# Row statistics of the first stage moved from VectorE to ScalarE, its biases and weights waited for at their use, and a large load held back

## The chip, the cores and the metric

The kernel runs on one core of a Trainium2 chip. The metric is the device time of one execution in microseconds (us). The core has five engines that run their own instruction streams and meet only through semaphores: PE (TensorE, matmul), DVE (VectorE), ACT (ScalarE), POOL (GpSimd) and SP, which here only issues DMA transfers. Each engine executes its stream in order, so an instruction that waits holds up all that stands behind it.

## The reference, cut to what matters

The model has four stages on x of 8 x 512 rows of 256. Only the first two are touched in more than bookkeeping, and the kernel runs both of them as one block, `first_layer`:

```python
x = x + tanh(g_xattn[0]) * L0_xattn(layernorm(x), ctx, ctx)
x = x + tanh(g_ffn[0])   * L0_ffn(layernorm(x))
x = x + tanh(g_xattn[1]) * L1_xattn(ctx, layernorm(x), mask)
x = x + tanh(g_ffn[1])   * L1_ffn(layernorm(x))

def layernorm(x):
    m = mean(x, -1); v = var(x, -1)
    return (x - m) / sqrt(v + 1e-5)

def L0_xattn(q, k, v):            # attention over the 16 heads of one row
    Q = (q @ Wq + bq).reshape(b, s, 16, 16)
    K = (k @ Wk + bk).reshape(b, s, 16, 16)
    V = (v @ Wv + bv).reshape(b, s, 16, 16)
    w = softmax(einsum('bsid,bsjd->bsij', Q, K) / 4)
    return einsum('bsij,bsjd->bsid', w, V).reshape(b, s, 256) @ Wo + bo
```

L0_ffn is a linear layer to 1024 with relu, rounded to 8 bits, and a linear layer back to 256.

## The kernel before, in words

The 4096 rows of x stand in SBUF as the tensor X, 32 tiles (NT) of 128 rows. `first_layer` works in rounds t = -3 to 38, and every engine's program is one loop over the rounds, written out by hand; semaphores count tiles. The order within a round, and how far one engine's round lies ahead of another's, decides who waits. In round t:

- ACT copies the projections of tile t+2 out of PSUM (`xT_copy`, `kv_copy`, `q_copy`, L454 to L468), copies the transposed result of tile t-1 (L472), takes the exponentials of tile t (`exp`, L477 and L478), normalises tile t+3 (L449), does the relu of the feed-forward part (L493), its results (L498 to L504), sums for the next stage (`next_statistics`, L438 to L442), and as the last thing `f_statistics(t - 1)` (L426 to L432): mean and variance of tile t-1 after its first update, by activations with an accumulated sum.
- POOL does `scores(t + 1)`: products of queries and keys in two instructions (L282, L284), in every odd round then `f_deviations` of a pair of tiles (L273, L275: variance to the power -0.5, and the mean times that), and one addition (L291). Then `weighted(t)` (L296), probabilities times values, for which it waits for `exp(t)`.
- DVE sums POOL's products of tile t-1 (L602, `other_values`) and scales them (L606, tensor `a_on`), takes the row maxima of tile t (L584, L586), makes its own share of products (L590, L597, L574, L578) and updates X (L612, L617).
- PE transposes and projects tile t+2 (`qkv`, L315 to L332), transposes `a_on` of tile t-1 (`turn_out`, L315), does the matmuls of the feed-forward part (L366, L377), the output projection (L342, L343), and adds up the scores of tile t+1 (L350 to L355).

POOL runs ahead of ACT: POOL's round t+1 begins as soon as `weighted(t)` is done, while ACT is still in its round t.

The first layernorm needs mean and variance of every tile of the unchanged X. Before, DVE made them in three portions as X landed (`x_stats`, L666 and L555 to L558: tiles 0 to 3, 4 to 15, 16 to 31), and POOL took each portion's power (`x_deviations`, L266, L268). X is loaded in the same three portions by SP (L201). SP issues, in this order: X part 0, four bias rows, context tile 0, the four weights wk, wv, wq, wo, context tile 1, X part 1 (1.5 MB), w1 and w2 (1 MB each), b1, b2, X part 2 (2 MB), and then the context tiles 2, 3 and so on, each held until PE has used the tile two before it (context tile 2: until `qkv(0)` has used tile 0). DVE splits the biases into three bf16 parts (`split_biases`), and ACT issues the transfer that puts the parts on three partitions (tensor bias3, L418). PE began only when all of `w_in` was there, the four weights and bias3.

Of the kernel before, what the change touches and what calls it, by code (L numbers as in the profile page):

```python
# [12 lines left out]
P = 128  # L13
BATCH, SEQ, D = 8, 512, 256
T = BATCH * SEQ
NT = T // P
# [68 lines left out]
def first_layer(nc, x, ctxT, mask, maskT, g_xattn, g_ffn, W, F0, L1, X, tg, ident_f, stats, mu_rs, xs_dram, ahead):  # L85
# [4 lines left out]
    with ExitStack() as ctx:  # L90
# [73 lines left out]
        act_chain, f_means = sem("act_chain"), sem("f_means")  # L164

# [28 lines left out]
        def _(sp):  # L194
# [21 lines left out]
            context(1)  # L216
            x_part(1)
# [32 lines left out]
        def _(pool):  # L250
# [18 lines left out]

            def f_deviations(b):  # L270
                pair = slice(2 * b, 2 * b + 2)
                pool.wait_ge(f_stats, 2 * b + 2)
                pool.tensor_tensor(mu_rs[:, 1, pair], eps_t[:, pair], half[:, pair], ALU.pow).then_inc(f_rstd, 1)  # L273
                pool.wait_ge(f_rstd, b + 1)
                pool.tensor_tensor(shift[:, pair], shift[:, pair], mu_rs[:, 1, pair], ALU.mult).then_inc(f_shift, 1)  # L275
# [24 lines left out]
            x_deviations(1)  # L300
            for t in ROUNDS:
                if t == 0:
                    x_deviations(2)
                if within(t + 1):
                    scores(t + 1, block_of(t, 3))
                elif block_of(t, 3) is not None:
                    f_deviations(block_of(t, 3))
                if within(t):
                    weighted(t)

        @block.tensor
        def _(pe):
# [5 lines left out]
            def qkv(t):  # L318
                pe.wait_ge(xn_done, t + 1)
                turn(xT_ps, ps_T, xn[t % 2], t)  # L320
                pe.wait_ge(c_in[t % 2], 16 * (t // 2 + 1))
                wait(pe, kv_sb, t)
                for c in range(KC):
                    mm = pe.matmul(ps_kv, cT[t % 2][:, c, :], wkv[:, c, :], start=(c == 0), stop=False)
                mm.then_inc(c_used, 1)
                pe.matmul(ps_kv, ones3[:, :], bias3[:, D:3 * D], start=False, stop=True).then_inc(kv_ps, 1)
                pe.wait_ge(xT_sb, t + 1)
                wait(pe, q_copied, t)
                wait(pe, own_made, t)
# [59 lines left out]
            pe.wait_ge(w_in, 5 * 16)  # L389
# [24 lines left out]
        def _(act):  # L414
            act.wait_ge(g_in, 32)
            act.activation(tg[:, :], gl[:, :], ACT.Tanh).then_inc(tanh_done, 1)
            act.wait_ge(bias_split, 1)
            act.dma_start(bias3[:, :], bias_parts[:, :, :]).then_inc(w_in, 16)  # L418
            act.wait_ge(tanh_done, 1)
            steps = Steps(act, act_chain)  # L420

            def f_statistics(t):

                act.wait_ge(y_used, t + 1)
                steps.wait()
                steps.done(act.activation(spare[:, :], X[:, t, :], ACT.Copy, accum_out=sums[:, t:t + 1]))  # L426
                steps.wait()
                steps.done(act.activation(shift[:, t:t + 1], sums[:, t:t + 1], ACT.Copy, scale=-1.0 / D))
                steps.wait()
                steps.done(act.activation(spare[:, :], X[:, t, :], ACT.Square, bias=shift[:, t:t + 1], accum_out=sums[:, t:t + 1]))  # L430
                steps.wait()
                act.activation(eps_t[:, t:t + 1], sums[:, t:t + 1], ACT.Identity, bias=epsilon[:, :], scale=1.0 / D).then_inc(f_stats, 1)  # L432
# [12 lines left out]
            def normalise(t):  # L445

                wait(act, shift_done, 1 + [t in tiles for tiles in PARTS_OF_X].index(True))
                wait(act, xT_ps, t - 1)
                act.activation(xn[t % 2][:, :], X[:, t, :], ACT.Identity, bias=shift[:, t:t + 1],  # L449
                               scale=mu_rs[:, 1, t:t + 1]).then_inc(xn_done, 1)  # L450
# [62 lines left out]
            for t in ROUNDS:  # L513
# [8 lines left out]
                if within(t + 3):  # L522
                    normalise(t + 3)
                if t == -1:
                    f_weights()
# [14 lines left out]
                if within(t - 1):  # L540
                    f_statistics(t - 1)

        @block.vector
        def _(dve):
# [81 lines left out]
            x_stats(1)  # L626
            dve.wait_ge(tanh_done, 1)
            for t in ROUNDS:
# [14 lines left out]
                if t == -2:  # L643
                    x_stats(2)
# [154 lines left out]
def cross_attention(nc, ctxT, mask, maskT, L1, M1, X, tg, ident_f, stats, mu_rs, kept, ahead, routing, xs, out):  # L799
# [3 lines left out]
    with ExitStack() as ctx:  # L803
# [83 lines left out]
        gate_in, x_out, tables = sem("gate_in"), sem("x_out"), sem("tables")  # L887
# [23 lines left out]
        CONSTS = 20  # L911
# [90 lines left out]
        def _(pool):  # L1002
# [5 lines left out]
            def constants():  # L1008
# [9 lines left out]
                pool.iota(iota_i[:, :], pattern=[[1, NE]], base=0, channel_multiplier=0).then_inc(tables, 1)  # L1018
                pool.iota(token[:, :], pattern=[[P, NT]], base=0, channel_multiplier=1).then_inc(tables, 1)
                pool.wait_ge(consts, 16)  # L1020
# [386 lines left out]
        def _(dve):  # L1407
# [118 lines left out]
            def gate_tables():  # L1526
                dve.wait_ge(tables, 2)
# [183 lines left out]
def experts(nc, M1, X, ident_f, routing, xs, out):  # L1711
# [10 lines left out]
    with ExitStack() as ctx:  # L1722
# [50 lines left out]
        with ExitStack() as run:  # L1773
# [49 lines left out]
            labelled, blanks, before_in = sem_("labelled"), sem_("blanks"), sem_("before_in")  # L1823
# [28 lines left out]
            def _(pool):  # L1852
# [34 lines left out]
                for p in range(2):  # L1887
                    pool.memset(yb[p][:, :, :], 0.0).then_inc(blanks, 1)
                pool.wait_ge(blanks, 2)
# [311 lines left out]
```

## Time and profile before

| | us |
|---|---|
| median of 3 runs | 2061.55 |
| lowest and highest | 2059.53, 2062.3 |
| the profiled execution | 2063.94 |
| its span (first to last instruction) | 2062.2 |
| first stage: start to the next stage's first matmuls | 0 to 515 |
| expert stage at the end, bound by PE | 1375 to 2062 |

Over the whole span PE is busy 92%, DVE 75%, ACT 56% and POOL 45%. These are means over stages that are bound by different engines, so they say nothing on the first stage; that is read from stretches of its own. In a row of the timeline the first number is the start from the beginning of the span, the second the length, both in us, and a bracket gives how long the engine was idle before and who released it. "x10" is a number of instructions merged in one row.

### The profile page before, as it was taken

The page shows a single profiled execution, that of the slowest core. Times are in us where ns is not written, and L with a number is a line of the kernel's source. Part 1 is how long each engine was busy: PE and PEld are TensorE (multiplying, and loading weights), DVE is VectorE, ACT ScalarE, POOL GpSimd, SP SyncE. Part 2 cuts the span into 40 slices and gives each one's busy share as a digit, 9 for nine tenths or more (in the row PEclk, how much of TensorE's full clock was granted, in tenths as well). Part 3 has the DMA queues.
Part 4 walks back from the last instruction along what each step waited for, and adds up shares of the span by engine and source line. Part 5 has one row for each costly group of instructions (what it writes and reads, how often), then busy time and mean ns, then how long its engine had stood idle before and what let it go on. Part 6 is the DMA issues. An engine that isn't in the chain of part 4 may idle for free. (4 is left out here: it accounts for less than half of the span.)

```text
span 2062.2 us, 35515 instructions
## 1 busy us (share of the span) xinstructions
PE 1892.7 (92%) x12100; PEld 1339.9 (65%) x12100; DVE 1552.3 (75%) x3251; ACT 1145.8 (56%) x2414; POOL 935.7 (45%) x674
## 2 busy tenths in 40 slices
PE   4899999986889999998999999959999999999998
PEld 2566776664543434443434343449999999999998
DVE  7999999992566677777767678657777777777785
ACT  2356666655336555555555555516665665656563
POOL 6999999981633334343534351023222231222322
PEclk9999999997999999999999999979999999999999
DMA  5222222210425051524242423037666666666662
GB/s 176 114 93 114 91 113 114 108 37 1 116 65 124 27 129 53 123 68 108 68 110 73 104 92 77 19 108 251 238 224 234 229 230 209 226 226 231 231 226 89
DMA packets 138569, 271.45 MB, mean 132 GB/s; under 512 B 13244, under 2 KB 90256, under 8 KB 132499
## 3 DMA queue, kind: packets, MB, share of 16 engines
q1 hardware_dynamic: 127916, 243.63, 37.9%
q0 software_dynamic: 9952, 25.25, 3.3%
q8 instruction: 99, 1.62, 0.3%
q14 instruction: 84, 0.68, 0.1%
q10 hardware_dynamic: 518, 0.27, 0.0%
HBM read 200.12 MB, written 70.47 MB: 131 GB/s over the span
## 5 line engine op out<-in xcount | busy, mean ns | idle before, releaser
L1476 DVE CUSTOM_DVE_ANT_0 x_dump<-x_ps,x_bias_q 128x512 bf16<-128x512 f32 x512 | 353.1, 690 | 103.0 <-PE x_ps L1160 90.1
L1345 ACT ACTIVATE x_PT<-x_ps 128x512 f32<-128x512 f32 x512 | 292.2, 601 | 230.6 <-PE x_ps L1175 227.4
L1989 ACT ACTIVATE X<-m_ps 128x256 f32<-128x256 f32 (+1 forms) x312 | 113.1, 363 | 222.0 <-PE m_ps L1918 219.6
L1160 PE MATMUL x_ps<-x_KS,x_QS 96*128 96x512 bf16 x512 | 198.1, 387 | 23.1 <-DVE x_mx L1476 22.2
L1872 POOL DMA_INDIRECT out_dram<-e_y,e_label x71 | 71.6, 1008 | 321.6 <-DVE e_y L2051 302.2
L1174 PE MATMUL x_ps<-x_bias_k,x_ident_b 128*128 128x512 bf16 x512 | 196.6, 384 | 2.8 <-DMA x_QS<-x_rows 1.7
L1175 PE MATMUL x_ps<-x_QS,x_KS 98*128 98x512 bf16 x512 | 196.5, 384 | 0.0
L1918 PE MATMUL m_ps<-e_x_lo,m_hi 128*128 128x256 f32 (+1 forms) x640 | 180.1, 281 | 4.5 <-issue 4.5
L1918 PE MATMUL m_ps<-e_x_hi,m_hi 128*128 128x256 f32 (+1 forms) x640 | 180.0, 281 | 0.0
L1918 PE MATMUL m_ps<-e_x_hi,m_lo 128*128 128x256 f32 (+1 forms) x640 | 179.9, 281 | 0.0
L2033 DVE TENSOR_TENSOR X<-X,m_ps 128x256 f32<-128x256 f32 (+1 forms) x312 | 114.0, 394 | 83.8 <-ACT X L1989 80.0
L1864 POOL DMA_INDIRECT e_y<-out_dram,e_label x71 | 101.8, 1434 | 164.8 <-DMA out_dram<-e_y,e_label 83.2
L296 POOL TENSOR_TENSOR a_pool_pv<-a_e,a_v 128x2304 f32<-128x2304 f32 x32 | 162.8, 5087 | 16.0 <-ACT a_e L478 16.0
L1918 PE MATMUL m_ps<-e_x_hi,e_hi 128*128 128x256 f32 (+1 forms) x608 | 169.8, 279 | 0.0
L1918 PE MATMUL m_ps<-e_x_hi,e_lo 128*128 128x256 f32 (+1 forms) x608 | 169.5, 279 | 0.0
L1918 PE MATMUL m_ps<-e_x_lo,e_hi 128*128 128x256 f32 (+1 forms) x608 | 169.5, 279 | 0.0
L1768 DVE TENSOR_TENSOR m_lo<-m_raw,m_hi 128x2048 fp32r<-128x2048 f32 x60 | 137.3, 2288 | 28.8 <-ACT m_hi L1764 28.8
L1768 DVE TENSOR_TENSOR e_lo<-m_raw,e_hi 128x2048 fp32r<-128x2048 f32 x57 | 130.4, 2287 | 26.8 <-ACT e_hi L1764 26.8
L1160 PEld LDWEIGHTS x_ps<-x_KS,x_QS 96*128 96x128 bf16 x512 | 50.1, 98 | 135.5 <-DVE x_mx L1476 104.9
L1918 PEld LDWEIGHTS m_ps<-e_x_lo,m_hi 128*128 128x128 f32 x640 | 121.8, 190 | 4.6 <-issue 4.6
L1918 PEld LDWEIGHTS m_ps<-e_x_hi,m_lo 128*128 128x128 f32 x640 | 121.8, 190 | 0.0
L1918 PEld LDWEIGHTS m_ps<-e_x_hi,m_hi 128*128 128x128 f32 x640 | 121.7, 190 | 0.0
(344 smaller groups left out, 5413.5 us busy)
## 6 DMA issues: line engine op xcount, KB each, us to landing
m_raw<-in_L_ffn_w_dram SPq DMA_DIRECT2D x117, 1024.0 KB, 5.1
expert_in<-a_blank SPq DMA_DIRECT2D x34, 1032.0 KB, 4.4
parts<-x_part SPq DMA_DIRECT2D x24, 512.0 KB, 3.8
m_x<-expert_in SPq DMA_DIRECT2D x32, 258.0 KB, 4.9
next_mask_k<-in_maskT_dram SPq DMA_DIRECT2D x32, 256.0 KB, 2.6
next_mask_q<-in_mask_dram SPq DMA_DIRECT2D x29, 256.0 KB, 2.8
x_KS<-parts SPq DMA_DIRECT2D x16, 384.0 KB, 11.3
x_QS<-parts SPq DMA_DIRECT2D x8, 576.0 KB, 6.7
```

The costliest lines, as they stand in the source:

```text
L296: pool.tensor_tensor(heads(pool_pv[:, :], PV_POOL), probabilities(e_[t % 2][:, PV_OWN * H:], PV_POOL), values(v_sb[t % 3][:, :], PV_POOL), ...
L1160: pe.matmul(ps_max[m % 2], QS[b % 2][0:HROWS, h, q * P:(q + 1) * P], KS[b % 2][0:HROWS, h, :], start=True, stop=True).then_inc(s1_ps, 1)
L1174: pe.matmul(ps_st[e % 3], ident_b[:, :], bias_k[b % 2][:, kc, :], start=True, stop=False)
L1175: pe.matmul(ps_st[e % 3], KS[b % 2][:, h, kc * P:(kc + 1) * P], QS[b % 2][0:HROWS + MROWS, h, :], start=False, stop=True).then_inc(st_read ...
L1345: act.activation(PT[unit % 2][:, k, :], ps_st[e % 3], ACT.Exp, scale=DH ** -0.5).then_inc(exp_done, 1)
L1476: dve.tensor_tensor_reduce(out=dump[:, :], in0=ps_max[m % 2], in1=bias_q[b % 2][:, q, :], scale=1.0, scalar=NEG, op0=ALU.add, op1=ALU.max, ...
L1768: eng.tensor_tensor(w_lo[p][n][:, :, :], raw[n][:, :, :], w_hi[p][n][:, :, :].bitcast(F32), ALU.subtract)\
L1864: pool.indirect_dma_start(out=yb[p][:, n, :], out_offset=None, in_=rows, in_offset=tokens(p, n), bounds_check=T - 1, oob_is_err=False).the ...
L1872: pool.indirect_dma_start(out=rows, out_offset=tokens(p, n), in_=yb[p][:, n, :], in_offset=None, bounds_check=T - 1, oob_is_err=False).the ...
L1918: mm = pe.matmul(out, left[a], right[b], start=first and n == 0, stop=last and n == 2)
L1989: act.activation(silu[f % 2][:, 0:wide], ps_h[f % 4][:, 0:wide], ACT.Silu).then_inc(silu_done, 1)
L2033: dve.tensor_tensor(gated[k % 2][:, n, 0:wide], silu[n][:, 0:wide], ps_h[f % 4][:, BLK:BLK + wide], ALU.mult)\
```

## The change

1. PE no longer waits for everything ahead of its loop. It waits for the four weights ahead of the first projection, and for bias3 (its own semaphore now, `bias3_landed`) ahead of the first matmul that uses it.
2. SP holds X part 1, and with it all that stands behind it in its order, until bias3 has landed.
3. DVE makes the statistics of tiles 0 to 3 only. Those of tiles 4 to 31 are made by ACT, tile t+6 as the last thing of round t, for t = -2 to 25 (`row_statistics`: the same four steps as `f_statistics`). POOL takes the power for a pair of tiles, t+4 and t+5, as the first thing of every even round 0 to 26 (`row_deviations`).
4. ACT issues the transfer of bias3 after it has normalised tile 0, where it was before it.
5. In the later stages some semaphores are merged (two iotas count as constants, two memsets count with the iotas).

```diff
@@ SP
             context(1)
+            sp.wait_ge(bias3_landed, 16)
             x_part(1)
@@ POOL
+            def row_deviations(b):
+                pair, n = slice(2 * b, 2 * b + 2), b - TPB // 2
+                pool.wait_ge(row_stats, 2 * n + 2)
+                pool.tensor_tensor(mu_rs[:, 1, pair], eps_t[:, pair], half[:, pair], ALU.pow).then_inc(rstd_done, 1)
+                pool.wait_ge(rstd_done, n + 2)
+                pool.tensor_tensor(shift[:, pair], shift[:, pair], mu_rs[:, 1, pair], ALU.mult).then_inc(shift_done, 1)
...
             x_deviations(0)
-            x_deviations(1)
             for t in ROUNDS:
-                if t == 0:
-                    x_deviations(2)
+                if t % 2 == 0 and TPB <= t + 4 < NT:
+                    row_deviations((t + 4) // 2)
                 if within(t + 1):
                     scores(t + 1, block_of(t, 3))
@@ PE, qkv(t)
+                if t == 0:
+                    pe.wait_ge(w_in, 4 * 16)
...
+                if t == 0:
+                    pe.wait_ge(bias3_landed, 16)
                 pe.matmul(ps_kv, ones3[:, :], bias3[:, D:3 * D], start=False, stop=True).then_inc(kv_ps, 1)
...
             pe.wait_ge(consts, 5)
-            pe.wait_ge(w_in, 5 * 16)
@@ ACT
-            act.wait_ge(bias_split, 1)
-            act.dma_start(bias3[:, :], bias_parts[:, :, :]).then_inc(w_in, 16)
...
+            def row_statistics(t):
+                act.wait_ge(x_in[[t in tiles for tiles in PARTS_OF_X].index(True)], 16)
+                act.wait_ge(f_means, 1)
+                statistics(t, row_stats)
...
             def normalise(t):
-                wait(act, shift_done, 1 + [t in tiles for tiles in PARTS_OF_X].index(True))
+                act.wait_ge(shift_done, 1 if t < TPB else t // 2 - TPB // 2 + 2)
...
+                if t == -3:
+                    act.wait_ge(bias_split, 1)
+                    act.dma_start(bias3[:, :], bias_parts[:, :, :]).then_inc(bias3_landed, 16)
...
                 if within(t - 1):
                     f_statistics(t - 1)
+                if TPB <= t + 6 < NT:
+                    row_statistics(t + 6)
@@ DVE
             x_stats(0)
             split_biases(4, bias_row, bias_rest, bias_parts)
-            x_stats(1)
...
-                if t == -2:
-                    x_stats(2)
```

The order on POOL, from `weighted` of an odd round through the even round behind it to the next odd one. Before:

```order
L296 TENSOR_TENSOR a_pool_pv<-a_e,a_v 128x2304 [waits a_pv_read,a_e_ready]
L282 TENSOR_TENSOR a_pool_qk<-a_q,a_k 128x1536 [waits a_s_ps,a_q_copied]
L284 TENSOR_TENSOR a_pool_qk<-a_q,a_k 128x1280
L291 TENSOR_TENSOR a_pool_qk<-a_pool_qk 128x1024 [waits a_b_made,a_a_made]
L296 TENSOR_TENSOR a_pool_pv<-a_e,a_v 128x2304 [waits a_pv_read,a_e_ready]
```

And in the changed kernel, in which L292, L294, L301 and L306 are these same lines:

```order
L306 TENSOR_TENSOR a_pool_pv<-a_e,a_v 128x2304 [waits a_pv_read,a_e_ready]
L276 TENSOR_TENSOR mu_rs<-a_eps,a_half 128x2 [waits a_row_stats]
L278 TENSOR_TENSOR a_shift<-a_shift,mu_rs 128x2 [waits a_rstd_done]
L292 TENSOR_TENSOR a_pool_qk<-a_q,a_k 128x1536 [waits a_s_ps,a_q_copied]
L294 TENSOR_TENSOR a_pool_qk<-a_q,a_k 128x1280
L301 TENSOR_TENSOR a_pool_qk<-a_pool_qk 128x1024 [waits a_b_made,a_a_made]
L306 TENSOR_TENSOR a_pool_pv<-a_e,a_v 128x2304 [waits a_pv_read,a_e_ready]
```

The pair's power now stands ahead of the scores, behind a wait for `row_stats`, which ACT raises at the end of its previous round.

The order on ACT at the end of an odd round, before:

```order
L438 ACTIVATE a_spare,a_sums<-X 128x256 [waits a_act_chain,a_f_used]
L440 ACTIVATE mu_rs<-a_sums 128x1 [waits a_act_chain]
L442 ACTIVATE a_spare,mu_rs<-X,mu_rs 128x256 [waits a_act_chain]
L426 ACTIVATE a_spare,a_sums<-X 128x256 [waits a_act_chain,a_y_used]
L428 ACTIVATE a_shift<-a_sums 128x1 [waits a_act_chain]
L430 ACTIVATE a_spare,a_sums<-X,a_shift 128x256 [waits a_act_chain]
L432 ACTIVATE a_eps<-a_sums,a_epsilon 128x1 [waits a_act_chain]
L454 ACTIVATE a_xnT<-a_ps 128x256 [waits a_xT_ps]
```

And in the changed kernel:

```order
L446 ACTIVATE a_spare,a_sums<-X 128x256 [waits a_act_chain,a_y_used]
L448 ACTIVATE a_shift<-a_sums 128x1 [waits a_act_chain]
L450 ACTIVATE a_spare,a_sums<-X,a_shift 128x256 [waits a_act_chain]
L452 ACTIVATE a_eps<-a_sums,a_epsilon 128x1 [waits a_act_chain]
L446 ACTIVATE a_spare,a_sums<-X 128x256 [waits a_act_chain,a_f_means,a_x_in1]
L448 ACTIVATE a_shift<-a_sums 128x1 [waits a_act_chain]
L450 ACTIVATE a_spare,a_sums<-X,a_shift 128x256 [waits a_act_chain]
L452 ACTIVATE a_eps<-a_sums,a_epsilon 128x1 [waits a_act_chain]
L474 ACTIVATE a_xnT<-a_ps 128x256 [waits a_xT_ps]
```

A second set of the four steps, on the unchanged tile t+6, stands between `f_statistics` and the next round's first copy.

The order of SP's transfers at the start is the same but for one wait:

```order
L207 DMA a_cT<-in_ctxT_dram 128x2x128
L202 DMA X<-in_x_dram 128x12x256 [waits a_bias3_landed]
L220 DMA a_w<-in_w1T_dram 128x2x1024
L221 DMA a_w<-in_w2T_dram 128x8x256
L222 DMA a_b1c<-in_b_dram 128x8
L223 DMA a_b<-in_b_dram 1x256
L202 DMA X<-in_x_dram 128x16x256
L207 DMA a_cT<-in_ctxT_dram 128x2x128 [waits a_c_used] x3
```

The wait in the second row is the new one; the last row begins with context tile 2.

## Rows read from the trace of the kernel before

**Rows 1.** Windows view, rounds 10 and 11: window, length, busy per engine, granted clock, DMA.

```profile
177.95:205.25 27.30, 26.08 (x142) 19.14 (x141) 26.13 (x25) 17.64 (x55) 25.84 (x10) 1.00 0.22 87
```

**Rows 2.** Timeline of POOL, rounds 9 to 11: start, length, instruction, [idle before <- releaser].

```profile
164.53 5.10 POOL L296 TENSOR_TENSOR a_pool_pv<-a_e,a_v 128x2304 f32<-128x2304 f32 x1
...
169.58 2.81 POOL L282 TENSOR_TENSOR a_pool_qk<-a_q,a_k 128x1536 f32<-128x1536 f32 x1
...
178.43 5.08 POOL L296 TENSOR_TENSOR a_pool_pv<-a_e,a_v 128x2304 f32<-128x2304 f32 x1 [1.22 <-ACT a_e L478]
...
188.55 0.70 POOL L273 TENSOR_TENSOR mu_rs<-a_eps,a_half 128x2 f32<-128x2 f32 x1
...
189.48 2.38 POOL L291 TENSOR_TENSOR a_pool_qk<-a_pool_qk 128x1024 f32<-128x1024 f32 x1
```

**Rows 3.** Timeline of DVE: rounds 10 and 11, the sum of POOL's products.

```profile
173.67 2.55 DVE L602 TENSOR_REDUCE a_ps<-a_pool_pv 128x144 f32<-128x2304 f32 x1
...
187.03 2.55 DVE L602 TENSOR_REDUCE a_ps<-a_pool_pv 128x144 f32<-128x2304 f32 x1
...
189.73 0.42 DVE L606 TENSOR_TENSOR a_on<-a_ps,a_rden 128x256 f32<-128x256 f32 x1
```

**Rows 4.** Timeline of ACT: statistics of round 9, first and last, and round 11's first.

```profile
171.39 0.42 ACT L426 ACTIVATE a_spare<-X 128x256 f32<-128x256 f32 x1
...
172.80 0.29 ACT L432 ACTIVATE a_eps<-a_sums,a_epsilon 128x1 f32<-128x1 f32 x1
...
186.48 0.36 ACT L454 ACTIVATE a_xnT<-a_ps 128x256 f32<-128x256 f32 x1
```

**Rows 5.** Timelines of POOL and ACT, round 25: the same two ends.

```profile
382.96 5.10 POOL L296 TENSOR_TENSOR a_pool_pv<-a_e,a_v 128x2304 f32<-128x2304 f32 x1
...
391.23 0.29 ACT L432 ACTIVATE a_eps<-a_sums,a_epsilon 128x1 f32<-128x1 f32 x1
```

**Rows 6.** Timeline of PE, rounds 10 and 11, around the wait for DVE.

```profile
176.85 0.44 PE L315 MATMUL a_ps<-ident_f,a_on 128*128 128x128 f32 x2 [0.69 <-DVE a_on L606]
...
179.49 0.28 PE L343 MATMUL a_ps<-a_bias,a_ones 3*128 3x256 bf16 x1
...
189.44 0.28 PE L332 MATMUL a_ps<-a_bias,a_ones 3*128 3x256 bf16 x1
...
190.21 0.44 PE L315 MATMUL a_ps<-ident_f,a_on 128*128 128x128 f32 x2 [0.49 <-DVE a_on L606]
```

**Rows 7.** Timeline of PE, rounds 5 and 6, and the granted clock there in the windows view.

```profile
107.53 0.44 PE L315 MATMUL a_ps<-ident_f,a_on 128*128 128x128 f32 x2 [1.46 <-DVE a_on L606]
...
111.76 0.28 PE L343 MATMUL a_ps<-a_bias,a_ones 3*128 3x256 bf16 x1
...
122.24 0.44 PE L315 MATMUL a_ps<-ident_f,a_on 128*128 128x128 f32 x2 [1.17 <-DVE a_on L606]
...
108.00:110.00 2.00, 2.00 (x12) 2.00 (x12) 1.67 (x2) 1.48 (x4) 1.92 (x3) 0.50 0.24 99
...
122.00:124.00 2.00, 1.76 (x15) 1.76 (x16) 1.60 (x4) 1.25 (x4) 1.85 (x2) 1.00 0.76 318
```

**Rows 8.** Timeline of all engines, the start of the kernel.

```profile
10.68 1.30 ACTq L418 DMA_DIRECT2D a_bias<-a_bias_parts  x1
...
16.23 0.66 PE L315 MATMUL a_ps<-ident_f,a_xn 128*128 128x128 f32 x2 [16.23 <-DMA a_bias<-a_bias_parts]
...
26.79 5.32 DVE L666 BATCH_NORM_STATS2 stats<-X 128x6 f32<-128x256 f32 x16 [0.86 <-DMA X<-in_x_dram]
...
33.11 1.88 PE L324 MATMUL a_ps<-a_wkv,a_cT 128*128 128x512 f32 x4
...
42.62 0.27 ACT L477 ACTIVATE a_ps<-a_sm 128x112 f32<-128x112 f32 x1 [3.33 <-DVE a_sm L586]
```

**Rows 9.** DMA view (KB, us from issue to landing), and windows view, last columns DMA share, GB/s.

```profile
next_bias<-a_next_parts SPq DMA_DIRECT2D x3, 1.5 KB, 1.7
...
12.00:22.00 10.00, 5.21 (x12) 2.34 (x12) 5.27 (x27) 2.16 (x6) 1.59 (x1) 1.00 1.08 362
```

More of the change, by code:

```diff
@@ L164, in first_layer @@
         act_chain, f_means = sem("act_chain"), sem("f_means")
+        bias3_landed, row_stats = sem("bias3_landed"), sem("row_stats")
         slices = lambda a, n: a.rearrange("p (d i j) -> p d i j", d=n, i=H)
@@ L416, in _, with statistics @@
             act.activation(tg[:, :], gl[:, :], ACT.Tanh).then_inc(tanh_done, 1)
-            act.wait_ge(bias_split, 1)
-            act.dma_start(bias3[:, :], bias_parts[:, :, :]).then_inc(w_in, 16)
             act.wait_ge(tanh_done, 1)
             steps = Steps(act, act_chain)
+            def row_statistics(t):
+                act.wait_ge(x_in[[t in tiles for tiles in PARTS_OF_X].index(True)], 16)
+                act.wait_ge(f_means, 1)
+                statistics(t, row_stats)
             def f_statistics(t):
                 act.wait_ge(y_used, t + 1)
+                statistics(t, f_stats)
+            def statistics(t, ready):
                 steps.wait()
@@ L431, in f_statistics @@
                 steps.wait()
-                act.activation(eps_t[:, t:t + 1], sums[:, t:t + 1], ACT.Identity, bias=epsilon[:, :], scale=1.0 / D).then_inc(f_stats, 1)
+                act.activation(eps_t[:, t:t + 1], sums[:, t:t + 1], ACT.Identity, bias=epsilon[:, :], scale=1.0 / D).then_inc(ready, 1)
             def next_statistics(t):
@@ L886, in cross_attention @@
         m_ready, m_free, inverted = sem("m_ready"), sem("m_free"), sem("inverted")
-        gate_in, x_out, tables = sem("gate_in"), sem("x_out"), sem("tables")
+        gate_in, x_out = sem("gate_in"), sem("x_out")
         g_stats, g_rstd, g_xn, g_xT, gap, e2_done = (sem(n) for n in ("g_stats", "g_rstd", "g_xn", "g_xT", "gap", "e2_done"))
@@ L909, in wait @@
                 eng.wait_ge(semaphore, count)
-        CONSTS = 20
+        CONSTS = 22
         block = ctx.enter_context(nc.Block())
@@ L1017, in constants @@
                 pool.memset(ones_b[:, :], 1.0).then_inc(consts, 1)
-                pool.iota(iota_i[:, :], pattern=[[1, NE]], base=0, channel_multiplier=0).then_inc(tables, 1)
-                pool.iota(token[:, :], pattern=[[P, NT]], base=0, channel_multiplier=1).then_inc(tables, 1)
-                pool.wait_ge(consts, 16)
+                pool.iota(iota_i[:, :], pattern=[[1, NE]], base=0, channel_multiplier=0).then_inc(consts, 1)
+                pool.iota(token[:, :], pattern=[[P, NT]], base=0, channel_multiplier=1).then_inc(consts, 1)
+                pool.wait_ge(consts, 18)
                 pool.affine_select(out=before_b[:, :], in_=ones_b[:, :], compare_op=ALU.is_gt, fill=0.0,
@@ L1526, in gate_tables @@
             def gate_tables():
-                dve.wait_ge(tables, 2)
+                dve.wait_ge(consts, CONSTS)
                 do(dve.tensor_copy(iota_e[:, :], iota_i[:, :]))
@@ L1822, in experts @@
             g_high, y_left, y_out = sem_("g_high"), sem_("y_left"), sem_("y_out")
-            labelled, blanks, before_in = sem_("labelled"), sem_("blanks"), sem_("before_in")
+            labelled, before_in = sem_("labelled"), sem_("before_in")
             passed = sem_("passed")
@@ L1887, in _ @@
                 for p in range(2):
-                    pool.memset(yb[p][:, :, :], 0.0).then_inc(blanks, 1)
-                pool.wait_ge(blanks, 2)
+                    pool.memset(yb[p][:, :, :], 0.0).then_inc(iotas, 1)
+                pool.wait_ge(iotas, 7)
                 for q in range(ROUND):
```

## The prediction

> **What bounds the kernel now.** The change lives in the first stage, so I read its stretches only. First the windows view over two of its rounds [rows 1]: of 27.30 us PE is busy 26.08, DVE 26.13, POOL 25.84 and ACT 17.64. Three engines are nearly full and ACT has room. Next the timelines of one pair, rounds 10 and 11. POOL sits idle 1.22 us once in the pair, ahead of `weighted(10)` [rows 2]. DVE starts the sum of tile 9 at 173.67 and that of tile 10 at 187.03 [rows 3], though POOL had finished these products at 169.63 and 183.51 [rows 2]: they lie ready for 4.0 and 3.5 us. So DVE sets the pace, and POOL is early by 3.5 us. Last, where ACT stands against POOL: the reader should see that POOL ends round 9 at 169.63, while ACT ends `f_statistics` of its round 9 at 173.09 [rows 2, 4]. In round 25 the same ends are 388.06 and 391.52 [rows 5]. POOL is ahead of ACT by 3.46 us both times, and in the odd rounds between.
>
> At the start the bound is another: PE waits until 16.23 for bias3, and the first exponentials run at 42.62 [rows 8].
>
> **The new wait on POOL (the main term).** In even round E, POOL's first instruction now needs the statistics of tile E+5, and these are the last work of ACT's round E-1. Take E = 10. ACT ends `f_statistics` at 173.09. The four steps took 171.39 to 173.09, 1.70 us [rows 4]; a second set right behind them adds about 1.65, since neighbouring activations overlap a little. It ends at 174.74. POOL has been free since 169.6, so it stands for 5.1 us. It then runs the pair's power, 188.55 to 189.48 or 0.93 us; the three score instructions, 169.58 to 177.21 (178.43 less the idle 1.22) or 7.63 us; and `weighted`, 5.08 us [rows 2]. With 0.06 us for the semaphore, `weighted(10)` ends at 188.44, and DVE starts summing at about 188.47 where it started at 187.03. So of 5.1 us of standing, 1.22 of old idle and the 3.5 of lead absorb most, less the 0.93 of new work, and 1.4 us is left on DVE, which has no slack of its own. ACT's end of the next odd round follows DVE's `a_on` (PE turns it, the output projection, the update, then ACT), so the delay is passed on and each even round adds its own 1.4. From round 8 to round 26 these are 10 rounds: **+14.1 us**. In rounds 0 to 6 the feed-forward part is not complete, ACT ends earlier, and I charge nothing. The bounds of this term: 0 if something lets ACT run ahead, 20 if the early rounds pay too.
>
> **The clock (a second term, from the first).** PE waits for `a_on` 0.69 us in round 10 and 0.49 in round 11 [rows 6]. With the change `a_on(10)` comes 1.4 later while PE's projections before it end at 189.72 [rows 6] plus about 0.15 (ACT's copy at 186.48 starts 1.65 later [rows 4]). The gap becomes 1.75 us. In round 5 a gap of 1.46 us was followed by a granted clock of 0.50, that is 1.2 instead of 2.4 GHz, and in round 6 one of 1.17 was not [rows 7]. With the slow clock, turning `a_on` to the end of the output projection took 107.53 to 112.04, 4.51 us; at the full clock 176.85 to 179.77, 2.92 us [rows 6, 7]. That is 1.6 us on PE ahead of the relu for which ACT waits, hence 1.6 us on ACT's end of the odd round, on which POOL now waits. Once it happens DVE and ACT fall back against POOL's wait and the gap of the next pair is longer. Odd rounds 9 to 25 are 9; I take 7 of them: **+11.2 us**. Bounds: 0 and 9 x 2.0 = 18. The Trainium skill (TensorE: Matmul & The Clock Gate, section "HAM oscillation — how this bites in real kernels") describes a loop whose wait in every tile throws the array back to the slow clock every time; by it all 9 rounds would pay, and the term would be 14.4.
>
> **The start.** ACT issues bias3 at 10.68 for 1.30 us; it landed only when the large loads had gone by, and PE began at 16.23 [rows 8]. Held back, they no longer compete: the smallest transfer of this kind took 1.7 us [rows 9], so it lands between 12.4 and 13.7, and I take 13.0. The Trainium skill (DMA: Bandwidth & Descriptors, "Anatomy of one DMA") gives about 2.0 us of fixed cost; by it the landing would be 12.7 and the sum 0.3 us lower.
> The price stands behind it on SP's queue. X part 1, w1, w2, X part 2 and context tile 2 are 5.9e6 bytes (1.5 + 1 + 1 + 2 + 0.125 times 1024 x 1024), and at the 362 GB/s of the full queues [rows 9] they take 16.3 us. With 13.0 and the 1.7 us that a small transfer takes by itself that is 31.0; for the issue of the first of them and the waits I add 1, and context tile 2 is there at 32. It used to follow X part 2, landed at 26.8 [rows 8]. So the first tiles gain 3 us and more from bias3, and then tile 2 waits for the transfer: PE projects it at 32 instead of 33.11 [rows 8]. But before, DVE's 16-tile statistics (5.32 us, then their aggregation) [rows 8] stood ahead of its scores, and held back PE's query projection of tile 2, the scores and `exp(0)`; that is gone. From this projection, 1.88 us for keys and values [rows 8] and about as much again for biases, queries and ACT's copies make an estimated 4 us at the full clock and 6.5 at the half; PE will have been idle, so I take 5.4. `exp(0)` at 37.5 against 42.62: **-5 us**. Bounds: -2 (slow clock and bias3 at 14) and -7 (full clock, quick landing). The 12-tile statistics also go from DVE, but ran while it waited for the first query projection: nothing. The merged semaphores of the later stages wait for work that was done just ahead anyway: nothing. The start of the next stage follows the end of this one, so the sum goes through in full.
>
> **Sum.** 14.1 + 11.2 - 5 = +20.3 us. Against the profiled execution, 2063.94 us with a span of 2062.2, that is 2084.2; it lay 2.4 over the median of the runs, so the forecast is 2061.55 + 20.3 = 2082.
>
> **Rivals.**
> - *A: POOL's wait without the clock.* The granted clock was 1.00 in rounds 10 and 11 [rows 1] and a gap of 1.17 did no harm; if 1.75 does none either, +14.1 - 5 = +9, 2071 us. Chance 0.27.
> - *B: the clock in all rounds and longer.* Each odd round pays 2.0 and the first pairs stand too: 18 + 18 - 3 = +33, 2094 us. Chance 0.12.
> - *C, the other side: the wait is covered.* If the last statistics come no later than 1.4 us sooner than I have them (POOL's wait below 3.7 us), DVE never waits, and only the start is left: 2061.55 - 5 = 2056.5 us. For it: ACT has 9.7 us of idle in a pair [rows 1]. Against: these idles lie elsewhere in the round, and from the relu to the end ACT runs without a gap. Chance 0.08.
> - *D: the two cancel.* Stall in few rounds, or ACT's idle taking in half of it, and a start of -7: within 0.2%. Chance 0.06.
> - The forecast, 20.3 us within 5 or so: chance 0.47.
>
> **How the numbers follow.** The time is that of the likeliest case. Its own range is 2077 to 2088. The range of 8 in 10 takes in A and stops short of B and of D: 2066 to 2092. A measurement of this kernel tells a change from none at about 0.2%, 4 us. Faster is C with a little of D, 0.09; the same 0.06; slower 0.85.
>
> **What would show it.** In the changed profile: POOL idle 5 us ahead of the power of a pair in every even round from 8 to 26, released by ACT's last statistics step; DVE idle 1.4 us or more ahead of its sum of POOL's products in the round behind; period of a pair 28.7 us or, with slow matmuls in odd rounds, 30.3, and 27.3 again after round 28; PE's gaps ahead of turning `a_on` near 1.75 us and granted clock below 1.00 in that stretch; bias3 landed at 13, context tile 2 at 32, `exp(0)` at 37 to 38. The forecast is wrong if POOL does not stand, if the odd rounds keep the full clock, or if `exp(0)` is not earlier.

## The result, and the profile after

| | before | after |
|---|---|---|
| median, us | 2061.55 (2059.28 to 2063.67, 5 runs) | 2078.60 (2076.12 to 2092.33, 5 runs) |
| ratio after/before | | 1.0096 (95% interval 1.0062 to 1.0129) |
| span of the profiled execution, us | 2062.2 | 2090.4 |
| sum of POOL's products of tile 8 starts | 159.72 | 155.79 |
| of tile 26 | 405.45 | 424.38 |
| of tile 31, the last | 469.14 | 490.54 |
| next stage's first matmul | 515.37 | 537.48 |

The change costs 17.0 us by the medians. (The ratio in the table would be 19.8 us; it takes in the one long execution of 2092.3.) The profiled execution of after is that long one, the slowest of its five (the others lie between 2076.1 and 2079.4), so its own surplus of 28 us isn't what is to be explained; the section on the prediction comes back to that. Inside the first stage the loss is plain: ahead by 3.9 us at tile 8, behind by 18.9 at tile 26 and by 21.4 at tile 31.

First the pair of rounds 10 and 11 after the change, the timeline of all engines. It answers to [rows 2, 3, 4, 6]. Columns: start, length, instruction, [idle before <- what ended it].

```profile
164.06 5.06 POOL L306 TENSOR_TENSOR a_pool_pv<-a_e,a_v 128x2304 f32<-128x2304 f32 x1
...
170.20 0.29 ACT L452 ACTIVATE a_eps<-a_sums,a_epsilon 128x1 f32<-128x1 f32 x1
...
171.79 0.29 ACT L452 ACTIVATE a_eps<-a_sums,a_epsilon 128x1 f32<-128x1 f32 x1
...
172.16 0.71 POOL L276 TENSOR_TENSOR mu_rs<-a_eps,a_half 128x2 f32<-128x2 f32 x1 [3.04 <-ACT a_eps L452]
...
180.71 5.06 POOL L306 TENSOR_TENSOR a_pool_pv<-a_e,a_v 128x2304 f32<-128x2304 f32 x1
...
185.81 2.56 DVE L627 TENSOR_REDUCE a_ps<-a_pool_pv 128x144 f32<-128x2304 f32 x1 [1.80 <-POOL a_pool_pv L306]
...
188.99 0.54 PE L324 MATMUL a_ps<-ident_f,a_on 128*128 128x128 f32 x2 [2.23 <-DVE a_on L631]
...
202.38 0.71 POOL L276 TENSOR_TENSOR mu_rs<-a_eps,a_half 128x2 f32<-128x2 f32 x1 [3.25 <-ACT a_eps L452]
```

Read it from the top. POOL has finished round 9 at 169.12. ACT ends the feed-forward statistics at 170.49 and the added ones at 172.08, and only then does POOL take the pair's power. `weighted(10)` ends at 185.77, and DVE, which before found these products lying ready for 3.5 us [rows 2, 3], waits 1.80 us for them. PE then waits 2.23 us for `a_on(10)`, where it waited 0.49 [rows 6]. From one power to the next it is 30.22 us; the pair took 27.30 [rows 1].

POOL is now held, and its standing adds straight to the pair: 30.22 less 3.25 of standing is 26.97, all of it its own instructions and their small gaps. Before it stood 1.22 us in a pair, for an `a_e`, with 3.5 us of lead. But no single engine sets the new pace. A ring does: POOL works from its power to the end of `weighted(10)` (172.16 to 185.81, 13.65 us, with the short step to DVE), DVE sums and scales (to 188.99, 3.18 us), PE turns `a_on(10)`, and PE and ACT carry it on to ACT's last statistics, for which POOL waits (to 202.38, 13.39 us). The three parts are the 30.22 us of the pair, so what lengthens any of them lengthens every pair.

The windows view of after: the pair, 2 us after PE's gap in round 11, 2 us after its gap in round 17, and round 27. It answers to [rows 1] and [rows 7]. Columns: window, length, busy of PE, PEld, DVE, ACT, POOL, granted clock, DMA share, GB/s.

```profile
172.16:202.38 30.22, 27.82 (x141) 20.52 (x140) 26.27 (x26) 20.57 (x66) 26.67 (x13) 0.94 0.20 80
...
189.00:191.00 2.00, 2.00 (x10) 2.00 (x11) 1.63 (x3) 1.42 (x4) 2.00 (x2) 0.55 0.15 58
...
279.70:281.70 2.00, 2.00 (x16) 1.96 (x17) 1.63 (x3) 1.58 (x5) 2.00 (x2) 1.00 0.02 8
...
427.00:429.00 2.00, 1.44 (x9) 1.44 (x10) 1.51 (x4) 0.93 (x4) 2.00 (x2) 0.78 1.01 421
```

The full clock of the pair [rows 1] has become 0.94: after the gap of 2.23 us the granted clock was 0.55, close to the lower level of 1.2 GHz. After the gap in round 17, which was 2.24 us long (row below), it stayed at 1.00. From sum to sum of the even tiles 8 to 26 the pairs last 30.02, 30.20, 30.24, 30.17, 28.68, 30.21, 30.19, 30.17 and 28.71 us: seven with the slow clock (0.94 over the whole pair) and two without.

The timeline of after once more, round 17 and, ahead of it, the start, which answers to [rows 8].

```profile
9.71 0.66 PE L324 MATMUL a_ps<-ident_f,a_xn 128*128 128x128 f32 x2 [9.71 <-ACT a_xn L469]
...
10.79 1.30 ACTq L546 DMA_DIRECT2D a_bias<-a_bias_parts  x1
...
12.79 0.37 SPq L202 DMA_DIRECT2D X<-in_x_dram  x1
...
13.94 0.60 PE L339 MATMUL a_ps<-a_bias,a_ones 3*128 3x512 bf16 x1
...
32.01 3.64 PE L335 MATMUL a_ps<-a_wkv,a_cT 128*128 128x512 f32 x4 [3.34 <-DMA a_cT<-in_ctxT_dram]
...
37.49 0.26 ACT L497 ACTIVATE a_ps<-a_sm 128x112 f32<-128x112 f32 x1
...
46.14 2.55 DVE L627 TENSOR_REDUCE a_ps<-a_pool_pv 128x144 f32<-128x2304 f32 x1
...
279.61 0.44 PE L324 MATMUL a_ps<-ident_f,a_on 128*128 128x128 f32 x2 [2.24 <-DVE a_on L631]
```

SP, which waits for bias3, issues X part 1 at 12.79. PE starts at 9.71 instead of 16.23, then has to wait for context tile 2 until 32.01, and projects it at the slow clock (3.64 us for what took 1.88 [rows 8]). The first exponentials run at 37.49, and the first sum of POOL's products at 46.14 instead of 51.55.

### The profile page after: what moved, and what is told of

Same layout as the page of the kernel before. It is cut to its first block and busy times, and to the rows that moved or that the text cites. A ratio compares the mean times of both kernels' runs of the same rounds, so it can differ in the third digit from the quotient of the medians.

```text
span 2090.4 us, 35676 instructions
## 1 busy us (share of the span) xinstructions
PE 1916.0 (92%) x12100; PEld 1353.0 (65%) x12100; DVE 1539.2 (74%) x3191; ACT 1188.2 (57%) x2582; POOL 939.2 (45%) x698
## 5 line engine op out<-in xcount | busy, mean ns | idle before, releaser
L306 POOL TENSOR_TENSOR a_pool_pv<-a_e,a_v 128x2304 f32<-128x2304 f32 x32 | 162.3, 5071 | 1.2 <-ACT a_e L498 1.2
L1078 POOL TENSOR_TENSOR x_rest<-x_full,x_part 128x512 f32<-128x512 f32 x28 | 32.4, 1159 | 201.9 <-ACT x_part L1355 201.9
## 6 DMA issues: line engine op xcount, KB each, us to landing
x_KS<-parts SPq DMA_DIRECT2D x16, 384.0 KB, 11.2
```

The source lines that it names most:

```text
L306: pool.tensor_tensor(heads(pool_pv[:, :], PV_POOL), probabilities(e_[t % 2][:, PV_OWN * H:], PV_POOL), values(v_sb[t % 3][:, :], PV_POOL), ...
```

## The experiments

All times are medians; a ratio is to the kernel before, measured beside it on the same chip. The first four experiments ran on one chip, where the kernel before took 2060.91 us, and the last four on another, where it took 2062.63. A difference to the changed kernel compares runs made at different times, so a few us of it mean little. Rounds, tiles and `sum(t)` (DVE's start on POOL's products of tile t) are as above.

**1. The power taken later (e1_power_later).** The changed kernel, but POOL takes the pair's power behind the two score products of the round.

```diff
-            def scores(t, block):
+            def scores(t, block, rows=None):
...
                 if block is not None:
                     f_deviations(block)
+                if rows is not None:
+                    row_deviations(rows)
                 pool.wait_ge(a_made, t + 1)
...
-                if t % 2 == 0 and TPB <= t + 4 < NT:
-                    row_deviations((t + 4) // 2)
+                rows = (t + 4) // 2 if t % 2 == 0 and TPB <= t + 4 < NT else None
                 if within(t + 1):
-                    scores(t + 1, block_of(t, 3))
+                    scores(t + 1, block_of(t, 3), rows)
```

> The changed kernel with one edit: in even rounds POOL takes the pair's power after its two score products instead of ahead of them. Theory (POOL's wait for ACT's last work of the round before is what costs): the products take 5.1 us, as long as POOL stood, so the wait is gone, DVE sets the pace again at 27.3 us a pair, PE's gap ahead of turning a_on is 0.5 to 0.7 us again and its clock stays up; only the start's gain is left, 2061.5 - 5 = 2056.5 us. Rival 1 (the added work costs: 1.65 us on ACT a round and 0.93 on POOL a pair): the pair stays at 28.7 or more, about 2075. Rival 2 (part of the loss is the later stages, not the first): 2063 or more although the pair is 27.3.

It took 2052.41 us, ratio 0.9958 (0.9944 to 0.9972): 26 us under the changed kernel, and under the kernel before. The timeline of POOL and ACT, round 10:

```profile
165.05 2.40 POOL L294 TENSOR_TENSOR a_pool_qk<-a_q,a_k 128x1280 f32<-128x1280 f32 x1
...
167.10 0.29 ACT L453 ACTIVATE a_eps<-a_sums,a_epsilon 128x1 f32<-128x1 f32 x1
...
167.47 0.71 POOL L276 TENSOR_TENSOR mu_rs<-a_eps,a_half 128x2 f32<-128x2 f32 x1
...
171.14 5.08 POOL L308 TENSOR_TENSOR a_pool_pv<-a_e,a_v 128x2304 f32<-128x2304 f32 x1 [0.36 <-ACT a_e L499]
```

The same instruction, 5.2 us later in POOL's program, waits for nothing: ACT ends at 167.39, POOL is there at 167.47. Only 0.08 us lie between, but 0.36 of old idle stands behind. The windows view of two of its rounds shows the old pair and the full clock, with all the added work in it:

```profile
165.78:193.10 27.32, 26.21 (x141) 19.11 (x140) 26.16 (x27) 20.61 (x67) 26.77 (x13) 1.00 0.22 88
```

So the loss is the place of the wait and not ACT's 3 us or POOL's 0.93 us of work in a pair. I had expected 2056.5, and it was better by 4. Of these the start gives 2.3 (`sum(8)` at 152.43, 7.3 us ahead of before, not 5), and most of that is the clock and not the edit: context tile 2 came as late as in the changed kernel (31.93), but PE projected it in 1.98 us instead of 3.64. The rest I can't place.

**2. The statistics one round earlier (e2_round_earlier).** The power stays in front; ACT takes the row statistics one tile further ahead.

```diff
-                if TPB <= t + 6 < NT:
+                if t <= 0 and TPB <= t + 6:
                     row_statistics(t + 6)
+                if t >= 0 and t + 7 < NT:
+                    row_statistics(t + 7)
```

> The changed kernel with ACT's row statistics one tile further ahead (tiles 6 and 7 both in round 0, from then on tile t+7 in round t); POOL's power stays the first instruction of the even round, and ACT and POOL do just the same work. Theory (the lead, not the work): the statistics are there a round before they are asked for, POOL does not stand, pair 27.3 us, 2056 to 2058 us. Rival (work): no better than the changed kernel, 2078. If it lies between, ACT's extra set in round 0 costs at the start.

2054.17 us, ratio 0.9965 (0.9950 to 0.9979). The timeline of ACT and POOL, rounds 8 to 10:

```profile
155.38 0.29 ACT L452 ACTIVATE a_eps<-a_sums,a_epsilon 128x1 f32<-128x1 f32 x1
...
165.57 0.71 POOL L276 TENSOR_TENSOR mu_rs<-a_eps,a_half 128x2 f32<-128x2 f32 x1
```

The last value that this power needs was made 9.9 us before, at the end of round 8. POOL takes the power at once, and from `sum(6)` on the pairs last 27.3. Two edits that share nothing but the lead of ACT over POOL remove the same loss.

**3. The clock kept (e3_clock_kept).** In odd rounds PE runs three matmuls more ahead of turning `a_on`, on a buffer that is overwritten afterwards; POOL's wait stays.

```diff
+                if t % 2 == 1 and 9 <= t <= 27:
+                    pe.wait_ge(h_act, FC * block_of(t, 5) + 4)
+                    for _ in range(3):
+                        pe.matmul(ps_h[:, 0:PAIR], ident_f[:, :], wkv[:, 0, 0:PAIR], start=True, stop=True)
```

> The changed kernel with three matmuls of the identity added on PE ahead of turning a_on, in the odd rounds 9 to 27, into a PSUM bank that is free there; their result is overwritten. They fill most of the gap in which PE waits. Theory (two terms, wait and clock): POOL still stands, all pairs take 28.7 us instead of 28.7 in two and 30.2 in seven, first stage ends about 11 us sooner than in the changed kernel, about 2067 us. Rival (the long pairs are not the clock's): pairs stay at 30.2 and the time at 2078, or longer by the matmuls.

2067.32 us, ratio 1.0036 (1.0022 to 1.0051), 11.3 us under the changed kernel. The timeline of POOL, DVE and PE, then the windows view of one pair:

```profile
169.68 0.71 POOL L276 TENSOR_TENSOR mu_rs<-a_eps,a_half 128x2 f32<-128x2 f32 x1 [1.69 <-ACT a_eps L456]
...
183.31 2.56 DVE L631 TENSOR_REDUCE a_ps<-a_pool_pv 128x144 f32<-128x2304 f32 x1 [1.28 <-POOL a_pool_pv L306]
184.69 1.56 PE L408 MATMUL a_ps<-a_wkv,ident_f 128*128 128x256 f32 x6
...
186.50 0.44 PE L324 MATMUL a_ps<-ident_f,a_on 128*128 128x128 f32 x2 [0.25 <-DVE a_on L635]
...
198.38 0.71 POOL L276 TENSOR_TENSOR mu_rs<-a_eps,a_half 128x2 f32<-128x2 f32 x1 [1.69 <-ACT a_eps L456]
```

```profile
183.31:212.00 28.69, 27.71 (x147) 20.14 (x146) 26.23 (x26) 20.74 (x66) 26.70 (x13) 1.00 0.21 84
```

The filler (the row of 1.56 us; the profile counts the three matmuls as six) stands where PE was idle, the clock is 1.00, and every pair from `sum(6)` to `sum(26)` lasts 28.7 us. POOL stands 1.69 us, and 28.69 less 1.69 is again 27.0. This divides the loss: POOL's wait makes 27.3 into 28.7, and the clock makes 28.7 into 30.2, through 1.55 us more of standing on POOL. In the ring only one part has changed. POOL's takes 13.63 us (169.68 to 183.31) and DVE's 3.19, as in the changed kernel, but from turning `a_on(10)` to the next power it is 11.88 (186.50 to 198.38) instead of 13.39: the slow clock costs 1.51 us on the way through PE and ACT.

**4. The wait alone (e4_wait_only).** The kernel before, and nothing added but a wait of POOL for ACT's feed-forward statistics of the round before.

```diff
+                if t % 2 == 0 and 2 <= t <= 26:
+                    pool.wait_ge(f_stats, t - 1)
                 if within(t + 1):
                     scores(t + 1, block_of(t, 3))
```

> The kernel before with one wait more and no work: in even rounds 2 to 26 POOL first waits until ACT has ended f_statistics of the round before. Theory: POOL stands 3.5 us in each from round 8 on, less than its 1.2 us of idle and the 3.5 us its products lie ready, so DVE never waits: 2061.5, same within 0.2%. The wait costs only from 4.7 us of standing on. Rival (every wait on POOL is passed on): 10 times 2 us or more, 2080.

2061.92 us, ratio 1.0008 (0.9994 to 1.0023): no change. The timeline of POOL and DVE, round 10:

```profile
173.63 2.80 POOL L282 TENSOR_TENSOR a_pool_qk<-a_q,a_k 128x1536 f32<-128x1536 f32 x1 [1.22 <-ACT a_eps L434]
...
181.23 5.07 POOL L296 TENSOR_TENSOR a_pool_pv<-a_e,a_v 128x2304 f32<-128x2304 f32 x1
...
187.49 2.55 DVE L604 TENSOR_REDUCE a_ps<-a_pool_pv 128x144 f32<-128x2304 f32 x1
```

POOL waits for ACT in each pair, yet DVE doesn't: the products end at 186.30, 1.2 us ahead of the sum, where they were 3.5 ahead [rows 2, 3]. The 3.5 us of standing that I expected didn't come: POOL stands 1.22 us in a pair, as before, only ahead of another instruction. Once it is held in each pair it isn't 3.5 us early at the next one. A wait that ends 1.65 us sooner (my estimate of ACT's second set) and carries no 0.93 of work behind it costs nothing. The threshold of rival C exists, and the change lies beyond it.

**5. The statistics alone (e5_statistics_only).** Only the move of the row statistics; bias3, PE's waits and SP's queue as before.

```diff
             context(1)
-            sp.wait_ge(bias3_landed, 16)
             x_part(1)
...
             act.activation(tg[:, :], gl[:, :], ACT.Tanh).then_inc(tanh_done, 1)
+            act.wait_ge(bias_split, 1)
+            act.dma_start(bias3[:, :], bias_parts[:, :, :]).then_inc(bias3_landed, 16)
...
             pe.wait_ge(consts, 5)
+            pe.wait_ge(w_in, 4 * 16)
+            pe.wait_ge(bias3_landed, 16)
```

> Part 3 of the change alone: the statistics on ACT and POOL as in the changed kernel, but the start as before (X part 1 not held, PE waits for weights and bias3 ahead of its loop, ACT issues bias3 first). Theory (pairs cost what the changed kernel's cost, and nearly all of the start's gain is DVE's freed statistics, not the bias): exp(0) between 31 and 38 us where the changed kernel has 37.5, pairs 28.7 to 30.2, total 2074 to 2079. Rival (the hold and the early bias make the gain): exp(0) near 42, total 2083.

2085.51 us, ratio 1.0107 (1.0087 to 1.0126), 7 us over the changed kernel. My expectation missed. The timeline of POOL, ACT and DVE at its start:

```profile
34.54 0.81 POOL L275 TENSOR_TENSOR mu_rs<-a_eps,a_half 128x2 f32<-128x2 f32 x1 [4.31 <-ACT a_eps L451]
...
36.67 0.41 ACT L497 ACTIVATE a_e<-a_sm 128x256 f32<-128x256 f32 x1
...
43.15 5.02 POOL L305 TENSOR_TENSOR a_pool_pv<-a_e,a_v 128x2304 f32<-128x2304 f32 x1
...
48.20 2.56 DVE L623 TENSOR_REDUCE a_ps<-a_pool_pv 128x144 f32<-128x2304 f32 x1 [3.01 <-POOL a_pool_pv L305]
```

The first exponentials are even a little earlier than in the changed kernel (36.67 against 37.67). But POOL gets its first power at 34.54 instead of 31.34, with `scores(1)` behind it, and `sum(0)` starts at 48.20 instead of 46.14. The new wait bites at the start too, and the first exponentials are not the measure of it. That gives 2.1 us; the first stage ends 2.0 us later than in the changed kernel, and its pairs are the same (30.11 to 30.24, and two of 28.70). The other 5 us of the 7 between the medians I can't place, and they may be none: the two were measured at different times, each beside its own runs of the kernel before, and the intervals of their ratios overlap (1.0087 to 1.0126 and 1.0062 to 1.0129). The profiled executions of the two stand the other way round (spans of 2085.7 and 2090.4).

**6. Experiment 1 without SP's wait for bias3 (e6_later_no_hold).**

```diff
-            sp.wait_ge(bias3_landed, 16)
```

> The kernel with the power taken behind the products (the first experiment, 2052.4 us), with SP's wait for bias3 ahead of X part 1 taken out. Theory (the hold costs, since context tile 2 queues behind all the held loads and exp(0) follows it): context tile 2 lands at 27 instead of 32, exp(0) runs at 31 to 33 instead of 35.8, total 2048. Rival (the hold helps, since bias3 lands at 16 without it and the first projections are 3 us later): exp(0) at 36 or later, total 2052 or more.

2053.57 us, ratio 0.9957 (0.9944 to 0.9970), the same as with the wait (0.9958). In the first stage it is ahead of experiment 1: `sum(0)` at 42.59 against 44.37, and the next stage's first matmul at 506.69 against 508.48. Here bias3 loses less by the large loads than they lose by being held. In the total the 1.8 us don't show.

**7. Experiment 1 with context tiles 2 and 3 ahead of X part 2 (e7_later_contexts_first).**

```diff
+            context(2)
+            context(3)
             x_part(2)
             for t in range(2, NT):
-                context(t)
+                if t > 3:
+                    context(t)
```

> The same kernel as in the first experiment, with context tiles 2 and 3 issued ahead of X part 2 (2 MB) instead of behind it. Theory (context tile 2 is what exp(0) waits for): it lands by 27, PE projects tile 2 as soon as it has added up the scores of tile 0, at 28.3, and ACT, busy with the weights' casts to 31.3, is the next to hold exp(0): at 33 to 34 instead of 35.8; total 2050. Rival (something else holds it): exp(0) stays at 35.8.

2051.03 us, ratio 0.9938 (0.9921 to 0.9956), the lowest median of all: 27.6 us under the changed kernel. From experiment 1, whose interval overlaps, it isn't told apart with certainty. Its timeline, PE and ACT at the start:

```profile
26.79 1.88 PE L339 MATMUL a_ps<-a_wkv,a_cT 128*128 128x512 f32 x4
...
33.13 0.26 ACT L501 ACTIVATE a_ps<-a_sm 128x112 f32<-128x112 f32 x1
```

Tile 2 is projected 5.2 us sooner than in the changed kernel, without a wait and at the full clock, and `exp(0)` comes 4.4 us sooner than there and 2.6 sooner than in experiment 1 (35.75).

**8. The start alone (e8_start_only).** Parts 1, 2 and 4 of the change: bias3 and the weights waited for at their use, SP held, bias3 issued after tile 0 is normalised. The row statistics stay on DVE and POOL, and the later stages are as before.

```diff
             context(1)
+            sp.wait_ge(bias3_landed, 16)
             x_part(1)
...
+                if t == 0:
+                    pe.wait_ge(w_in, 4 * 16)
...
+                if t == 0:
+                    pe.wait_ge(bias3_landed, 16)
...
+                if t == -3:
+                    act.wait_ge(bias_split, 1)
+                    act.dma_start(bias3[:, :], bias_parts[:, :, :]).then_inc(bias3_landed, 16)
                 if t == -1:
                     f_weights()
```

> Parts 1, 2 and 4 of the change alone: the statistics stay on DVE and POOL as in the kernel before. Theory (the held X parts now stand ahead of DVE's statistics, and those ahead of its scores): DVE's 12 tiles run at 19.8 to 25, its scores of tile 0 behind them, the 16 tiles at 31.5 to 38, exp(0) at 45 to 48 instead of 42.6, pairs 27.3, total 2064 to 2067. Rival (the early bias gains by itself): exp(0) near 39, total 2058.

2065.73 us, ratio 1.0018 (1.0004 to 1.0032). The timeline of DVE and ACT at the start:

```profile
19.63 4.02 DVE L672 BATCH_NORM_STATS2 stats<-X 128x6 f32<-128x256 f32 x12 [8.93 <-DMA X<-in_x_dram]
...
31.34 5.33 DVE L672 BATCH_NORM_STATS2 stats<-X 128x6 f32<-128x256 f32 x16 [2.61 <-DMA X<-in_x_dram]
...
47.17 0.27 ACT L480 ACTIVATE a_ps<-a_sm 128x112 f32<-128x112 f32 x1 [3.31 <-DVE a_sm L592]
```

With the loads held, DVE waits for X, and its 16-tile statistics start at 31.34 instead of 26.79 [rows 8]: `exp(0)` is 4.6 us later than before. Of that 3.4 us are left at `sum(8)`. By themselves these three parts of the change lose; they gain only together with the statistics taken off DVE. At `sum(0)` the statistics alone are 3.35 us ahead of before (experiment 5), and all parts together 5.41. Part 5, the merged semaphores, was not run alone.

## Why the prediction was right, and where it wasn't

- **The new wait on POOL, +14.1.** Right in place, cause and size: from `sum(7)` to `sum(26)` experiment 3, which keeps the clock up, takes 14.0 us more than before (273.03 against 259.07). A pair without the clock's part lasts 28.7 us in experiment 3 and twice in the changed kernel, 1.4 over the 27.3 before, in the ten even rounds 8 to 26; from experiment 1 to experiment 3, which differ in the place of the wait and the filler, it is 14.9 us. Experiments 1, 2 and 4 show that it is the lead that counts. One reading of it was wrong: I said that POOL would stand 5.1 us in every pair. It stands 1.7 us, or about 3.2 where the clock falls (2.56 and 3.04 in the first two of these pairs). I had reckoned 5.1 against a POOL that is 3.46 us ahead of ACT. Once it is held it no longer gets that far ahead, and 5.1 less 3.46 is the 1.7 that is seen. The delay handed on was right all the same, since lead and old idle were taken off.
- **The clock, +11.2.** Right in mechanism and near in size: seven of nine pairs paid 1.5 us, and from `sum(7)` to `sum(26)` the changed kernel takes 10.3 us more than experiment 3. (The 11.3 us between the two medians hold the start and the tail as well.) That it would be seven of nine I had from no row: the count was luck. I forecast gaps of 1.75 us, growing once the clock has fallen, and so they did. The first (for tile 8) was 1.75 and the one behind each pair at full clock 1.73 and 1.88 (tiles 18 and 26), the others 2.2. The loop of the Trainium skill (TensorE: Matmul & The Clock Gate, section "HAM oscillation — how this bites in real kernels"), in which each round pays, would have given 14.4; two rounds of this trace didn't pay, at gaps as long as the others (last section).
- **The tail, 0.** Too low. The gap for tile 26 (1.88 us) brought the clock down in round 27 too (0.78 in the windows above). From `sum(26)` to `sum(28)` it took 28.42 us and not 27.3, and 1.4 us more came by the last tile: +2.5. These 1.4 us can't be charged to POOL's wait. From `sum(29)` to `sum(30)` the granted clock was 0.73 where it was 0.85 before, and it was 0.73 too, with the same 1.2 us or more, in experiments 4 and 8, in which DVE doesn't wait for POOL once behind tile 0.
- **The start, -5.** Right in size and in its steps: context tile 2 at 32.01 (forecast 32), `exp(0)` at 37.49 (37.5), and 5.4 us ahead at `sum(0)`. bias3 landed by 12.79, 2.0 us after its issue at 10.79, where I had taken 2.3. The 2.0 us that the prediction quotes from the Trainium skill (DMA: Bandwidth & Descriptors, section "Anatomy of one DMA") agree with that, though the section is on transfers issued by GpSimd and ACT issues this one. The 5.4 us from context tile 2 to `exp(0)` were a choice between 4 at the full and 6.5 at the slow clock, and that they came out is in part luck. In experiments 1 and 3, whose edits don't touch these rounds' PE work, the same wait of 3.3 us was followed by a projection of 1.98 us instead of 3.64, and `exp(0)` was there 3.8 us after the tile, at 35.7. The reason I gave for bias3's part doesn't hold either, since experiments 6 and 8 show that the hold by itself costs. And I hadn't seen why `exp(0)` was quite so late before: DVE's low half of the first feed-forward weights, right ahead of the first softmax, took 4.39 us instead of the 2.28 it takes now (last section). The sum isn't touched by that, because it starts from the measured 42.62; after the change DVE is done with it at 30.83, ahead of context tile 2.
- **The sum, +20.3.** The first stage of the profiled execution ends 21.4 us later: -5.3 up to tile 7, +24.2 from there to tile 26 (forecast 25.3) and +2.5 in the tail. By the medians it is +17.0. The sentence that the sum goes through in full is true of the start of the next stage (+22.1), but the second stage doesn't last equally long each time. From its first matmul to the expert stage's first cast the profiled executions took 871.3 us before, 877.2 after, and between 866.1 and 873.6 in the experiments, none of which changes its work. Before's 871.3 lies 3 to 5 us over the five shortest (866.1 to 868.4). A forecast from one profiled execution is uncertain by these 3 to 5 us at least.
- **From one execution to another.** The granted clock goes with the difference between executions. Added up over windows of 5 us, the second stage ran about 37 to 42 us at the lower level in the five shortest executions and 45 to 58 us in the five others, after's 58 being the most. Take off half of that time as an estimate of what it cost, and all ten last 846 to 849 us. The long profiled execution of after fits this: its mean granted clock is 0.963, that of the other four 0.968 to 0.970, and span times clock, an estimate of the length at full clock, is 2010 to 2014 us in all five. Why the clock falls more often in one execution than in another stays open, and so does how the 17 us of the medians divide over the stages, since only the profiled execution has a trace.
- **The rivals.** A (no clock, 2071) falls by the granted clock of 0.55 and by experiment 3, B by the two pairs at the full clock and by rounds 2 to 6, where POOL stood 1.28 us at most and DVE didn't wait for it; C by DVE's 1.80 us of idle.

## What to carry to other kernels

When work is moved to an engine with room, the room is not the question: look at when its result is ready against when the reader's in-order queue comes to it. Here the same work, read 5 us later in that queue or made a round earlier, turned a loss of 17 us into a gain of 7 to 8.5. If the wait closes a ring of engines, the pair lasts as long as the ring, and every delay in it counts in full. Where the delay opens a gap on PE, look at the granted clock after it: it took the price of a pair from 1.4 us to 2.9.

## What the runs showed of the hardware

**DVE and POOL side by side.** The timeline of the kernel before, then of the changed kernel, at the instructions of DVE and POOL that met at the start:

```profile
36.85 2.79 POOL L282 TENSOR_TENSOR a_pool_qk<-a_q,a_k 128x1536 f32<-128x1536 f32 x1
...
37.40 4.39 DVE L647 TENSOR_TENSOR a_w_lo<-a_w,a_w_hi 128x2048 fp32r<-128x2048 f32 x1
...
39.60 4.41 POOL L284 TENSOR_TENSOR a_pool_qk<-a_q,a_k 128x1280 f32<-128x1280 f32 x1
```

```profile
28.55 2.28 DVE L669 TENSOR_TENSOR a_w_lo<-a_w,a_w_hi 128x2048 fp32r<-128x2048 f32 x1
...
35.05 2.35 POOL L294 TENSOR_TENSOR a_pool_qk<-a_q,a_k 128x1280 f32<-128x1280 f32 x1
```

Two of them are recorded with nearly twice the length that they have alone, 4.39 against 2.28 us and 4.41 against 2.35. Yet they overlap for 2.2 us only, and the ends show that they took turns. DVE's instruction began 0.55 us into POOL's first product, which wasn't lengthened, and ended 2.15 us after that product's end (39.64 to 41.79). POOL's second product ended 2.22 us after DVE's end (41.79 to 44.01). Each did its work in about the time that it needs alone, once the other was done, and the wait is inside the recorded length. The Trainium skill (SBUF — State Buffer, section "SBUF: two separate sides") says that VectorE with two inputs in SBUF and GpSimd share a port pair as an exclusive lock, which the one that starts first holds for its whole instruction. This trace agrees with that. That the port is the cause was not tested by itself.

**PE's gap and the clock.** The granted clock in the 2 us from the start of turning `a_on`, windows view of the changed kernel:

| tile | 8 | 10 | 12 | 14 | 16 | 18 | 20 | 22 | 24 | 26 |
|---|---|---|---|---|---|---|---|---|---|---|
| PE's gap, us | 1.75 | 2.23 | 2.16 | 2.20 | 2.24 | 1.73 | 2.17 | 2.17 | 2.23 | 1.88 |
| granted clock | 0.50 | 0.55 | 0.68 | 0.80 | 1.00 | 0.59 | 0.72 | 0.85 | 1.00 | 0.64 |

The length of the gap alone doesn't decide: the longest, 2.24 us, left the clock up, and in the kernel before one of 1.46 brought it down and one of 1.17 didn't [rows 7]. The row has an order, though. From pair to pair less of the 2 us is at the lower level, until the fall is missed once and it begins anew. Experiment 5 has its two full-clock pairs at the same places (tiles 16 to 18 and 24 to 26). What sets this order was not tested.
